# A ring of four pairs of places in a graph kernel's tile loop, with one subtraction and one row sum moved to other engines

## The chip, the cores and the metric

The kernel runs on one core of a Trainium2 chip. A core has five engines that run their own instruction streams and meet only in semaphores: PE (TensorE, matrix multiplications), DVE (VectorE), ACT (ScalarE), POOL (GpSimd) and SP (SyncE, which here only starts DMAs). PE multiplies out of SBUF into PSUM, which has eight banks; DVE and ACT bring results from PSUM back to SBUF. The metric is the time of one execution on the device, in microseconds (us), the median of several.

## The reference

Four graph layers one after the other on 3125 nodes with 128 features and 100,000 edges, sorted by destination. Layer 0 averages neighbours with edge weights in both directions, layer 1 applies the weighted adjacency three times, layer 2 the unweighted one four times, layer 3 is a message network over all edges.

```python
dst = jnp.minimum((3125 * uniform(100000) ** 2.0).astype(int32), 49999)   # sorted; crowded at the low end
...
m = ft[src] * w[:, None]                      # layer 0, both directions
msum = segment_sum(m, dst, num_segments=n); wsum = segment_sum(w, dst, num_segments=n)
...
Yk = segment_sum(edge_val[:, None] * X[edge_col], edge_row, num_segments=n)   # layer 1
...
agg = segment_sum(x[row], col, num_segments=n)                                # layer 2
```

The kernel never gathers rows for layers 0 to 2. It first builds the 3125 x 3125 matrix of edge weights (`adj`) and the matrix of edge counts (`cnt`) on the chip, and then multiplies with them. The change is in this first stage, the build.

## The kernel before

**What the build does.** Columns (destinations) are cut into 25 blocks of 125, and each block into 10 windows of 12 or 13 destinations in turn; 250 windows in all. The edges come in tiles of 128. For each tile, DVE makes two matrices by comparing an index row with a value per partition: `lanes` (L640), 128 x 128, which holds in one float both a 1 and the third part of the edge weight, and `keys` (L642), 128 x 300 or 325, a one-hot row in bf16. ACT scales `lanes` by the weight's first two parts into `scaled` (L685). PE then multiplies four times: the counts (L748), the third part of the weights (L752), and the other two parts (L756, twice), each 128 x 128 against 300 or 325 columns. All tiles of a window add up in two PSUM banks, one for counts and one for weights.

**How many tiles.** Each window has one first tile (place 0) and then a loop with a number of turns known only at run time (L514 on DVE and ACT, L543 on PE); each turn is one pair of tiles (places 1 and 2). There are 1132 tiles: 250 first ones and 441 pairs. Since destinations crowd at the low end, block 0 has 82 pairs, its first window alone 24; from block 13 on nearly every window has one pair.

**Places.** Before, even and odd windows have three places each (`SLOTS = 6`), and every place has its own `lanes`, `scaled` and `keys`. DVE may fill a place again once PE has given it free (`s_free`, raised by the last of the four multiplications). So within one window DVE is never more than two tiles ahead of PE.

**After a window.** ACT takes the counts out of PSUM as bf16 (`high`, L697) and the weights as float (L699). A count may not fit in one bf16, so PE subtracts `high` again from the PSUM bank with a multiplication by minus the identity (`rest`, L764), and ACT takes out what is left (`low`, L704), two windows behind. **After a block**, within the next block's windows: PE transposes `adj` in seven groups (L776, windows 1 to 7), which ACT copies out (L713, five groups) or DVE (L628, windows 3 and 7); PE multiplies `adj` with the node features (L784, windows 1 to 8); and DVE sums the rows of `adj` in five parts (`row_sums`, L649). SP stores the results to DRAM. POOL has nothing to do in the build.

Every engine runs the windows in the same written order; nothing is scheduled at run time but the number of turns. The blocks' loop is written out eight blocks long and turned three times.

## Time and profile before

| | us |
|---|---|
| median of 3 runs (lowest to highest) | 4106.24 (4103.90 to 4116.88) |
| span of the profiled execution | 4131.5 |
| build in it, from PE's first tile to its last | 51.0 to 1108 |
| matmul busy time, all stages | 3483.2 (84%) |
| DVE, ACT, POOL busy time | 1463.3, 1265.5, 871.1 |

For the profiled execution the trace gives its span alone, no time of its own around it; it is 25 us above the median of the runs. The page gives shares over the whole span, but the build is a stage with its own limits, so it is read in stretches, cut at block boundaries. "PEld" is PE's loading of weights; "issue" is time in which an engine waited for nothing that the profile shows, among it register and branch instructions. Such instructions are not counted as busy, but the view of one line lists them, with the letter q behind the engine (DVEq, PEldq), their number and their durations.

### The profile page before, as it was taken

Reading aid. Unit: us, or ns where it says so; the run is one execution under the profiler, and the core shown is the slowest. Engines: PE = TensorE matmul, PEld = TensorE weight load, DVE = VectorE, ACT = ScalarE, POOL = GpSimd, SP = SyncE. Lnnn points to the kernel's source line nnn. Section 1 sums busy time; section 2 is a strip of 40 time slices with the busy share of each in tenths; the row PEclk is TensorE's granted clock in tenths of the full one; section 3 lists DMA queues with packets and bytes.
Section 4 is the critical chain, followed back from the end, with each engine's and each line's share of the span. In section 5 each row is a group of like instructions: output and inputs, shape, how many; then the busy total and the mean of one; then the engine's idle time right before and its main releaser. Section 6 shows DMA issues by size and latency. Waiting matters only on the chain. (4 is left out here: it accounts for less than half of the span.)

```text
span 4131.5 us, 85615 instructions
## 1 busy us (share of the span) xinstructions
PE 3483.2 (84%) x23502; PEld 2445.5 (59%) x23503; DVE 1463.3 (35%) x4278; ACT 1265.5 (31%) x4012; POOL 871.1 (21%) x928
## 2 busy tenths in 40 slices
PE   5888889999988888968999999997777677776777
PEld 2345556777744434435999999985444445444545
DVE  6766667777601200024431111132222222222223
ACT  5566667878701300014322211232000000000001
POOL 2000000000010000000000000024666566666663
PEclk8999999999999999997999999997777778787778
DMA  2011222333495589861432222341222222222222
GB/s 60 1 46 62 69 70 87 106 101 119 133 231 127 136 188 230 196 169 31 124 107 78 76 77 77 89 115 48 65 63 63 60 63 63 62 63 63 61 63 55
DMA packets 120056, 381.79 MB, mean 92 GB/s; under 512 B 33166, under 2 KB 74620, under 8 KB 106026
## 3 DMA queue, kind: packets, MB, share of 16 engines
q1 hardware_dynamic: 90958, 324.81, 29.5%
q0 software_dynamic: 25664, 51.90, 5.7%
q8 instruction: 145, 2.38, 0.3%
q10 hardware_dynamic: 3154, 1.60, 0.2%
q14 instruction: 135, 1.11, 0.1%
HBM read 294.59 MB, written 83.62 MB: 92 GB/s over the span
## 5 line engine op out<-in xcount | busy, mean ns | idle before, releaser
L2266 POOL DMA_INDIRECT edge_rows<-src_table,src_idx x784 | 776.6, 991 | 471.2 <-issue 193.4
L685 ACT ACTIVATE build_scaled<-build_lanes,w 128x128 f32<-128x128 bf16 x1132 | 428.6, 405 | 307.4 <-DVE build_lanes L640 275.0
L756 PE MATMUL build_ps<-build_keys,build_scaled 128*128 128x300 bf16 (+1 forms) x2264 | 492.2, 299 | 20.5 <-ACT build_scaled L685 17.8
L640 DVE TENSOR_SCALAR build_lanes<-key_id,lane,one_w 128x128 f32<-128x128 f16 x1132 | 389.1, 344 | 237.9 <-PE build_ps L756 181.9
L2410 ACT ACTIVATE edge_act<-edge_ps 128x512 f32<-128x512 f32 x196 | 116.9, 597 | 1147.6 <-remote 741.7
L2382 PEld LDWEIGHTS edge_ps<-edge_hot,edge_act 128*128 128x128 f32 x1760 | 297.8, 244 | 263.5 <-issue 261.5
L1108 PE MATMUL prop_ps<-prop_rows,y 125*128 125x500 f32 (+1 forms) x1050 | 408.3, 546 | 50.0 <-DMA prop_rows<-adj_rows 43.2
L2360 PE MATMUL edge_ps<-m_store,edge_hot_t 125*128 x2640 | 269.1, 249 | 205.0 <-issue 126.0
L748 PE MATMUL build_ps<-build_keys,build_lanes 128*128 128x300 bf16 (+1 forms) x1132 | 345.3, 305 | 87.8 <-DVE build_keys L642 65.4
L642 DVE TENSOR_SCALAR build_keys<-key_id,key,win_base 128x300 bf16<-128x300 f16 (+1 forms) x1132 | 406.0, 359 | 0.5 <-issue 0.2
L2382 PE MATMUL edge_ps<-edge_hot,edge_act 128*128 x1760 | 316.3, 332 | 94.8 <-issue 58.9
L2360 PEld LDWEIGHTS edge_ps<-m_store,edge_hot_t 125*128 x2640 | 196.8, 110 | 269.2 <-issue 250.9
L1108 PEld LDWEIGHTS prop_ps<-prop_rows,y 125*128 125x128 f32 x1050 | 187.9, 191 | 269.2 <-issue 195.0
L752 PE MATMUL build_ps<-build_keys,build_lanes 128*128 128x300 bf16 (+1 forms) x1132 | 336.9, 298 | 0.0
L2368 PE MATMUL edge_ps<-edge_rows,ident 128*128 128x512 f32 x392 | 290.0, 829 | 28.7 <-issue 28.6
L756 PEld LDWEIGHTS build_ps<-build_keys,build_scaled 128*128 128x128 bf16 x2264 | 186.5, 98 | 158.4 <-ACT build_scaled L685 69.2
L748 PEld LDWEIGHTS build_ps<-build_keys,build_lanes 128*128 128x128 bf16 x1132 | 111.4, 98 | 227.0 <-DVE build_keys L642 181.2
L422 POOL DMA_DIRECT2D prop_work<-L_gnn_Wq_b_dram x1 | 0.8, 772 | 1090.3 <-POOLq L84 1090.3
L2307 DVE SCALAR_TENSOR_TENSOR edge_hot<-dst,block_base,edge_lane_id 128x500 f32 x220 | 162.8, 740 | 186.2 <-issue 177.6
L2286 DVE TENSOR_TENSOR m_agg_t<-m_agg_t,edge_ps x221 | 62.6, 283 | 459.3 <-remote 380.9
L2297 DVE TENSOR_SCALAR edge_hot_t<-edge_dst_row,block_base,edge_lane 125x512 int16 x220 | 92.6, 421 | 306.0 <-issue 176.0
L784 PE MATMUL build_ps<-h,build_adj 125*125 125x129 f32 x1250 | 173.3, 275 | 0.0
(368 smaller groups left out, 4762.4 us busy)
## 6 DMA issues: line engine op xcount, KB each, us to landing
prop_rows<-adj_rows SPq DMA_DIRECT2D x85, 1367.2 KB
cnt_panels<-build_cnt SPq DMA_DIRECT2D x50, 683.6 KB
adj_rows<-build_adj_t SPq DMA_DIRECT2D x25, 1367.2 KB
n<-cnt_panels SPq DMA_DIRECT2D x40, 683.6 KB
orders_panel<-cnt_panels SPq DMA_DIRECT2D x40, 683.6 KB
edge_dst_row<-dst_rows SPq DMA_DIRECT2D x196, 125.0 KB
h<-cnt_panels SPq DMA_DIRECT2D x20, 683.6 KB
prop_rows<-adj_rows SPq DMA_DIRECT2D x85, 158.7 KB
```

Of the source, the lines that this page charges most:

```text
L640: v.tensor_scalar(lanes[s][:], g.key_id[:, 0:128], g.lane[:, at], g.one_w3[:, at], ALU.is_equal, ALU.mult).then_inc(s_lanes[s], 1)
L642: v.tensor_scalar(keys[s][:, 0:KW[q] + q], g.key_id[:, 0:KW[q] + q], g.key[:, at], g.win_base[:, q, bass.ds(e, 1)], ALU.subtract, ALU.is_e ...
L685: a.activation(scaled[s][:], half(lanes[s], 1), ACT.Copy, scale=g.w12[:, bass.ds(t, 1)]).then_inc(s_scaled[s], 1)
L748: done = pe.matmul(ps[:, count_bank(j, parity), 0:KW[j % 2]], half(lanes[s], 1), keys[s][:, 0:KW[j % 2]], start=first, stop=False, skip_gr ...
L752: pe.matmul(ps[:, weight_bank(j), 0:KW[j % 2]], half(lanes[s], 0), keys[s][:, 0:KW[j % 2]], start=first, stop=False, skip_group_check=True)
L756: last = pe.matmul(ps[:, weight_bank(j), 0:KW[j % 2]], half(scaled[s], i), keys[s][:, 0:KW[j % 2]], start=False, stop=False, skip_group_ch ...
L784: last = pe.matmul(ps[0:B, N1, 0:D + 1], adj[parity][0:B, k, :], g.h[:, k, :], start=k == 0, stop=k == NB - 1)
L1108: last = pe.matmul(ps[:, c, 0:n * B], (y[0:B] if h else g.h)[:, row, 0:D], rows[row % R][:, b0 * B:(b0 + n) * B], start=at == 0, stop=at = ...
L2266: pool.indirect_dma_start(rows[s][:, i, :], None, dr.table, bass.IndirectOffsetOnAxis(ap=g.src_idx[:, t:t + 1], axis=0)).then_inc(s_rows[s ...
L2360: last = pe.matmul(ps[:, s, i * 128:(i + 1) * 128], hot_t[:, bass.ds(here, 1), i * 128:(i + 1) * 128] .rearrange("p a k -> p (a k)"), a3.q ...
L2368: pe.matmul(ps[:, s, :], g.ident[:], rows[s][:].rearrange("p a k -> p (a k)"), start=False, stop=True, skip_group_check=True).then_inc(s_p ...
L2382: last = pe.matmul(bank, act[s][:, i, :], hot[:, bass.ds(here, 1), i * B:(i + 1) * B].rearrange("p a k -> p (a k)"), start=i == 0, stop=i ...
```

## The change

Places 1 and 2 of the loop become a ring of four pairs that even and odd windows share: the tensors of places 1 and 2 are four times as wide, one counter goes on over all windows, and its two low bits, times 128 or 326 elements, are added to the address at run time. The first tiles keep a fixed place each for even and odd windows. The semaphore that frees a place starts at 4. `rest` on PE and `low` on ACT go; DVE instead subtracts `high` from the PSUM bank straight into the second bf16 part, behind its tiles of the window two further on. DVE's row sums go; POOL adds each finished block of `adj` to an array of 125 x 3125, and DVE sums that once at the end.

```diff
@@ build_phase
-        SLOTS = 6
-        lanes = [ph.sb(f"lanes{s}", [128, 128]) for s in range(SLOTS)]
...
+class Places:
+    def __init__(self, ph, depth):
+        self.depth = depth
+        self.lanes = [ph.sb(f"lanes{i}", [128, 128 * (depth if i > 1 else 1)]) for i in range(4)]
+        self.scaled = ...
+        self.keys = [ph.sb(f"keys{i}", [128, KEVEN * (depth if i > 1 else 1)], BF16) for i in range(4)]
+    def of(self, eng, q, place, n):
+        i = q if place == 0 else 1 + place
+        at = None if place == 0 else eng.snap(n & (self.depth - 1))
+        return i, at
...
+        SLOTS, DEPTH = 4, 4
@@ vector
-                    s = 3 * q + place
+                    s, r = places.of(v, q, place, n)
                     v.wait_ge(s_free[s], n)
-                    v.tensor_scalar(lanes[s][:], g.key_id[:, 0:128], ...
+                    v.tensor_scalar(places.wide(places.lanes[s], r), g.key_id[:, 0:128], ...
-            def row_sums(f, parity, i):
...
+            def low(w, j, parity):
+                v.wait_ge(s_high, w + 1)
+                v.tensor_tensor(in_block(cnt[parity][1], j), in_psum(count_bank(j, parity), j),
+                                in_block(cnt[parity][0], j), ALU.subtract).then_inc(s_low, 1)
...
                     spans.tiles(d, j, parity, one(j % 2, e))
+                    if j >= 2 or parity is not None:
+                        low(d * WPB + j - 2, *before(d, j, parity, 2)[:2])
...
-            v.tensor_reduce(g.wsum_src[:], rowsum[:].rearrange("p f h -> p h f"), AX.X, ALU.add)
+            v.tensor_reduce(g.wsum_src[:], by_lane[:], AX.X, ALU.add)
@@ gpsimd (new)
+            def block_of(d, parity, pair):
+                pool.wait_ge(s_weight, d * WPB + WPB)
+                pool.tensor_tensor(by_lane[:], by_lane[:], adj[parity or 0][0:B], ALU.add).then_inc(s_sum, 1)
+                pool.wait_ge(s_sum, d + 2)
+            pool.memset(by_lane[:], 0.0).then_inc(s_sum, 1)
@@ scalar
-            def low(w, j, parity):
-                a.wait_ge(s_rest, w + 1)
-                a.activation(in_block(cnt[parity][1], j), in_psum(count_bank(j, parity), j), ACT.Copy)...
@@ tensor
-                    s, first = 3 * (j % 2) + place, place == 0
+                    (s, r), first = places.of(pe, j % 2, place, n), place == 0
+                    moving = places.key(places.keys[s], r, KW[j % 2])
...
-                pe.matmul(in_psum(count_bank(j, parity), j), minus[:], in_block(cnt[parity][0], j), ...
-                pe.sem_inc(s_free[s], 1)
+                pe.sem_inc(s_free[s], DEPTH if s > 1 else 1)
```

What stands in the loop body on PE before, one turn (one pair of tiles) of an odd window. ISA and REGISTER_ALU are register instructions of PE's instruction stream; the others are as in the lines above.

```order
L55 ISA
L748 MATMUL build_ps<-build_keys,build_lanes 128x325 [waits build_keys4]
L752 MATMUL build_ps<-build_keys,build_lanes 128x325
L756 MATMUL build_ps<-build_keys,build_scaled 128x325 [waits build_scaled4]
L756 MATMUL build_ps<-build_keys,build_scaled 128x325
L748 MATMUL build_ps<-build_keys,build_lanes 128x325 [waits build_keys5]
L752 MATMUL build_ps<-build_keys,build_lanes 128x325
L756 MATMUL build_ps<-build_keys,build_scaled 128x325 [waits build_scaled5]
L756 MATMUL build_ps<-build_keys,build_scaled 128x325
L543 REGISTER_ALU
L543 COMPARE_AND_BRANCH
```

The first tile of the pair in the same place now; the second has one ISA and three REGISTER_ALU more, so a turn has ten register instructions that it did not have.

```order
L762 REGISTER_ALU [waits build_keys2]
L762 ISA x2
L762 MATMUL build_ps<-build_keys,build_lanes 128x325
L766 ISA
L766 MATMUL build_ps<-build_keys,build_lanes 128x325
L770 REGISTER_ALU [waits build_scaled2]
L770 MATMUL build_ps<-build_keys,build_scaled 128x325
L770 REGISTER_ALU
L770 MATMUL build_ps<-build_keys,build_scaled 128x325
L762 ISA [waits build_keys3]
```

The waits now stand at register instructions ahead of the multiplications. On DVE, one turn in an even window before:

```order
L640 ISA [waits build_free1]
L640 TENSOR_SCALAR build_lanes<-key_id,lane,one_w 128x128
L642 REGISTER_ALU
L642 TENSOR_SCALAR build_keys<-key_id,key,win_base 128x300
L640 ISA [waits build_free2]
L640 TENSOR_SCALAR build_lanes<-key_id,lane,one_w 128x128
L642 REGISTER_ALU
L642 TENSOR_SCALAR build_keys<-key_id,key,win_base 128x300
```

And now:

```order
L658 REGISTER_ALU [waits build_free2]
L658 ISA
L658 TENSOR_SCALAR build_lanes<-key_id,lane,one_w 128x128
L660 ISA
L660 TENSOR_SCALAR build_keys<-key_id,key,win_base 128x300
L658 ISA [waits build_free3]
L658 TENSOR_SCALAR build_lanes<-key_id,lane,one_w 128x128
L660 ISA
L660 TENSOR_SCALAR build_keys<-key_id,key,win_base 128x300
```

DVE has one register instruction more in a turn, and two of another kind; the number of its tile instructions is the same.

## Rows read from the trace of the kernel before

**Rows 1.** Whole blocks of the build: stretch, length, busy us (number) of PE, PEld, DVE, ACT...
```profile
51.00:191.50 140.50, 119.98 (x705) 47.26 (x706) 105.22 (x350) 77.23 (x209) 0.00 (x0) 0.98 0.01 4
191.50:327.00 135.50, 116.33 (x771) 63.58 (x772) 95.14 (x314) 82.15 (x242) 0.00 (x0) 1.00 0.14 47
327.00:616.90 289.90, 249.38 (x1687) 152.04 (x1688) 194.51 (x634) 185.88 (x574) 0.00 (x0) 1.00 0.20 66
616.90:757.70 140.80, 131.55 (x925) 92.72 (x925) 98.69 (x317) 103.32 (x328) 0.00 (x0) 0.98 0.28 91
757.70:1107.90 350.20, 338.21 (x2490) 262.59 (x2490) 257.61 (x818) 289.20 (x920) 0.00 (x0) 0.99 0.34 109
```

**Rows 2.** Timeline inside one window's loop: start, us, engine, line, [idle before <-releaser].
```profile
151.20 0.35 DVE L640 TENSOR_SCALAR build_lanes<-key_id,lane,one_w 128x128 f32<-128x128 f16 x1 [0.36 <-PE build_ps L756]
...
151.88 0.31 PE L748 MATMUL build_ps<-build_keys,build_lanes 128*128 128x325 bf16 x1 [0.26 <-DVE build_keys L642]
...
153.45 0.31 PE L748 MATMUL build_ps<-build_keys,build_lanes 128*128 128x325 bf16 x1 [0.24 <-DVE build_keys L642]
```

**Rows 3.** Register instructions of PE, by line: number, ns min/median/max, first and last start.
```profile
L543 PEldq COMPARE_BRANCH  x2: 215/215/215, 151.2 to 152.8; - x2
L532 PEldq FUSED_REGOPS  x122: 194/223/224, 50.6 to 1100.9; - x122
L2360 PEldq FUSED_REGOPS  x7: 46/46/51, 3006.8 to 3007.7; - x7
```

**Rows 4.** Timeline of PE at the start of block 21.
```profile
996.02 0.30 PE L748 MATMUL build_ps<-build_keys,build_lanes 128*128 128x300 bf16 x1
...
999.03 0.44 PE L764 MATMUL build_ps<-build_cnt,build_minus 128*128 128x325 bf16 x1
999.27 0.63 PE L776 MATMUL build_ps<-ident,build_adj 125*125 125x125 f32 x4
999.74 0.30 PE L748 MATMUL build_ps<-build_keys,build_lanes 128*128 128x325 bf16 x1
...
1000.85 1.05 PE L784 MATMUL build_ps<-h,build_adj 125*125 125x129 f32 x8
1001.74 0.29 PE L748 MATMUL build_ps<-build_keys,build_lanes 128*128 128x300 bf16 x1
```

**Rows 5.** The same stretch on ACT.
```profile
997.65 0.45 ACT L699 ACTIVATE build_adj<-build_ps 128x325 f32<-128x325 f32 x1
```

**Rows 6.** DVE and POOL in the setup: two timelines of one stretch.
```profile
18.57 0.61 DVE L321 TENSOR_SCALAR setup_blk<-setup_src_t 128x896 f32<-128x896 f32 x1
19.21 2.19 DVE L322 TENSOR_SCALAR setup_blk<-setup_blk 128x896 f32<-128x896 f32 x1
...
18.71 2.22 POOL L372 TENSOR_TENSOR setup_ea_left<-ea_raw,setup_ea_part 128x896 f32<-128x896 f32 x1
```

**Rows 7.** DVE's groups of the build by shape: busy us, mean ns | idle us before.
```profile
L640 DVE TENSOR_SCALAR build_lanes<-key_id,lane,one_w 128x128 f32<-128x128 f16 x1121 | 385.2, 344 | 233.8 <-PE build_ps L756 178.9 <-issue 50.4
L642 DVE TENSOR_SCALAR build_keys<-key_id,key,win_base 128x326 bf16<-128x326 f16 x561 | 203.6, 363 | 0.5 <-issue 0.2
L642 DVE TENSOR_SCALAR build_keys<-key_id,key,win_base 128x300 bf16<-128x300 f16 x561 | 198.8, 354 | 0.0
L649 DVE TENSOR_REDUCE build_rowsum<-build_adj 125x625 f32 x120 | 95.7, 797 | 0.0
```

**Rows 8.** Nearest rows for the two new operations: number, ns min/median/max.
```profile
L1334 POOL TENSOR_TENSOR x<-x,qk_half_b x1: 6950/6950/6950, 1857.9 to 1857.9; 125x3200 f32<-125x3200 f32 x1
...
L2286 DVE TENSOR_TENSOR m_agg_t<-m_agg_t,edge_ps x221: 276/284/290, 2865.3 to 4111.9; - x111
```

**Rows 9.** Waits of 616.9 to 1107.9 us: us in total, times, longest.
```profile
DVE build_adj_t L628 <- PE build_ps L776: 67.8, 26, 4.3
```

**Rows 10.** PE where the blocks' loop turns back, and the clock (third number from the end) behind it.
```profile
616.80 0.43 PE L748 MATMUL build_ps<-build_keys,build_lanes 128*128 128x300 bf16 x1 [4.25 <-issue]
...
618.00:621.00 3.00, 3.00 (x12) 1.54 (x11) 0.96 (x4) 0.40 (x1) 0.00 (x0) 0.50 0.00 0
```

More of the change, by code:

```diff
@@ L501, in __init__ @@
         self.now = [eng.alloc_register(name=f"span_now{k}") for k in range(2)]
-        self.pairs = [Counter(eng) for side in range(2)]
+        self.pairs = Counter(eng)
         eng.load(self.regs, g.spans[0:1, 0:4])
@@ L514, in tiles @@
         with self.eng.Fori(lo + 1, end, 2) as t:
-            n = self.pairs[j % 2].next()
+            n = self.pairs.next()
             one(1, t, n)
@@ L526, in __init__ @@
         self.now = eng.alloc_register(name="count_now")
-        self.pairs = [Counter(eng) for side in range(2)]
+        self.pairs = Counter(eng)
         eng.load(self.regs, g.counts[0:1, 0:4])
@@ L543, in tiles @@
         with self.eng.Fori(0, pairs):
-            n = self.pairs[j % 2].next()
+            n = self.pairs.next()
             one(1, n)
@@ L721, in block_of @@
                         out_of_psum(w - 1, jb, pb, db if parity is not None else None, pair)
-                    if j >= 2 or parity is not None:
-                        low(w - 2, *before(d, j, parity, 2)[:2])
                     if parity is not None:
@@ L732, in _ @@
             out_of_psum(NW - 1, WPB - 1, 0, None, None)
-            for j in (WPB - 2, WPB - 1):
-                low(NW - WPB + j, j, 0)
             for i in MOVES[1]:
@@ L807, in after_first @@
                     def after_first():
-                        if j >= 2 or parity is not None:
-                            rest(w - 2, *before(d, j, parity, 2)[:2])
                         if parity is not None:
@@ L825, in _ @@
             pe.drain().then_inc(s_opened, 1)
-            for j in (WPB - 2, WPB - 1):
-                rest(NW - WPB + j, j, 0)
             for j in range(1, WPB):
```

61 lines of the change are left out of this document (25 added, 36 removed).

## The prediction

> **What bounds the kernel now.** I read the busy shares in 40 slices first: in the build DVE and ACT are busy for 6 to 8 tenths and PE for 8 to 9, so none is full. Then the build in stretches of whole blocks [rows 1]. Matmuls there are four per tile, one `rest` per window and, but for the first stretch, 75 per block (25 transposes, 50 of L784). So 705 are 174 tiles; 771, 150; 1687, 294; 925, 146; 2490, 368. Less one first tile per window and halved, that is 82, 65, 117, 53 and 124 pairs, in 10, 20, 60, 40 and 120 windows.
>
> *A window with many pairs* is bound by a circle, not by an engine: DVE waits 0.36 us for PE to free a place, and PE waits 0.26 us for the keys made in it. From one pair to the next it is 151.88 to 153.45, 1.57 us for two tiles [rows 2]. Eight matmuls alone need 1.11 us (999.74 to 1000.85) [rows 4]. A ring is meant to break this circle.
>
> *A window with one pair*, as nearly all are from block 13 on, is bound by PE: 12 matmuls at 0.139 us, 1.6 to 1.7 us; on average 2.5 transposes at (0.63 - 0.27)/3 = 0.12 and 5 of L784 at (1.05 - 0.27)/7 = 0.11, 0.27 being one matmul's own time, together 0.85; and `rest` 0.24 (999.03 to 999.27) [rows 4]. That is 2.75 us; the stretch gives 350.2/120 = 2.92 [rows 1].
>
> **Part 1: the ring.** It takes the circle away, so PE gets its tiles in time. But what comes next is PE's own instruction stream. The loop body gains ten register instructions per turn. Their price: in the edge stage seven of them, and a short ALU_OP of the same line among them, start from 3006.8 to 3007.7 while PE multiplies beside them [rows 3]: seven steps, 0.13 us each. Of the ten, six are short ones, so I take 0.12. A body of 11 of them is 11 x 0.12 = 1.32 us. Turning back costs the loop's own ALU_OP and a branch of 0.215 us: from 152.8 to the next turn's first instruction some 0.3, together 0.37 us [rows 3]. A turn is 1.69 us, against 1.57 now and 1.11 of matmuls. So where a window is long the ring loses 0.12 us per turn, and where it has two or three turns it gains, since today each window also pays a start and a filling of its places.
>
> Outside the body a window has seven to eight register instructions (0.9 us), one or two of them long (0.223 against 0.046 us [rows 3]), and a register load every fourth window: 1.15 us, taken as unhidden; 0.95 in block 0. The bounds of the 0.12: 0.09, one short ALU_OP behind another, gives a body of 1.0 us, under which matmuls bound (1.11); if each of the five address ISAs took as long as L532, 0.9 us more per turn. I stay at 0.12, since L2360's are addresses for matmuls as well.
>
> PE's time by this, turns x 1.32 + turns beyond a window's first x 0.37 + windows x 1.15:
> - block 0: 108.2 + 26.6 + 9.5 = 144.3, now 140.5: +4.
> - blocks 1 to 2: 85.8 + 16.7 + 23 = 125.5, and 1 for stalls; now 135.5: -9.
> - blocks 3 to 8: 154.4 + 21.1 + 69 = 244.5, now 289.9. The blocks' loop turning back stays: 4.25 us and the half clock after it [rows 10], 5 together.
> - blocks 9 to 12: 70 + 4.8 + 46 = 120.8, and 2 for the clock; now 140.8.
> - blocks 13 to 24: a window is 1.15 + 1.32 = 2.47 by the stream and 2.5 by the matmuls; windows with transposes 2.7; I take 21.0 us for the eight windows 2 to 9.
>
> **Part 2: `rest` off PE, `low` from ACT to DVE.** PE saves 0.24 us x 250, all of it inside the numbers above, and it counts only where matmuls bind. ACT loses 250 copies; nothing waits for it then. DVE's subtraction reads 300 or 325 elements from PSUM. Between 284 ns for 125 elements [rows 8] and 797 for 625 [rows 7], 1.03 ns per element, it is 0.46 us; bounds 0.28 and 0.80. Ten per block are 4.6 us, against 5 x 0.8 = 4.0 of row sums that go. It stands behind DVE's tiles and waits for ACT's `high`, which came two windows earlier: at nothing, hidden in DVE's waits.
>
> **Part 3: the sum on POOL.** POOL itself is free. An addition of 125 x 3200 took 6.95 us [rows 8], so one of 3125 takes 6.8, 25 times, inside a block of 28 us or more. The price is what it does to DVE. In the setup the same DVE instruction took 0.61 us alone and 2.19 right after, its end (21.40) 0.47 us behind the end of POOL's addition (20.93) [rows 6]: DVE stood still until POOL was through. The tile instructions are of that kind (TENSOR_SCALAR, SBUF to SBUF), and their 128 x 326 takes only 9 ns more than 128 x 300 [rows 7], far under the 1 ns per element above. So I let POOL hold DVE for 6.8 us once per block. Bounds: nothing, if 16-bit tiles are not held, and 6.8 us on the path in each block.
>
> The Trainium skill states this as a rule (SBUF — State Buffer, "Who interferes with whom"): a DVE instruction in a mode with two ports and a GpSimd instruction exclude each other for a whole instruction, and `tensor_scalar` can enter such modes. By that rule, too, all 2264 tile instructions can be held; the trace agrees with 2.19 against 0.61 us.
>
> The hold begins when ACT has taken out a block's last weights. At block 21 that was 998.10, 2.1 us after PE opened window 0 [rows 4, 5]. With DVE ahead, PE has windows 0 and 1 to work on and then waits for window 2's keys: opening at 0, POOL from 2.0 to 8.8, keys and PE at 9.3. A block with single pairs is 9.3 + 21.0 = 30.3 us against 350.2/12 = 29.2 now. With two pairs per window the work ahead is 8 us long and hides the hold but for 1.5 us; blocks 9 to 12 lie between, 2.2 each. DVE's time for two pairs is 50 x 0.53 + 4.6 + 2.5 + 6.8 = 40.4 us, just under PE's 41. So:
> - blocks 3 to 8: 244.5 + 5 + 9 = 258.5: -31.
> - blocks 9 to 12: 122.8 + 8.8 = 131.6: -9.
> - blocks 13 to 24: 12 x 30.3 + 4 more pairs 3.6 + turning back 5.7 = 373: +23.
>
> Start and end: POOL's memset of the new array can hold DVE's first tiles, +2. The final sum over 3125 elements is about 3.3 us at 1.03 ns, beside the last stores: nothing. Clock: after 4.25 us of idleness PE ran at the lower of its levels, 1.2 GHz (0.50) [rows 10]. The new stalls of 3 to 4 us are near that; if one in three of twelve does it and costs 3 us, +12.
>
> **The sum:** 4 - 9 - 31 - 9 + 23 + 2 + 12 = -8 us. That stands against the profiled span of 4131.5 and would make 4123.5 there. The span is 25 us above the median of the runs, so in runs 4106 - 8 = 4098.
>
> **The rivals.**
> - *POOL doesn't hold the tile instructions.* For it: the row that shows a hold is of fp32 operands, the tiles read 16 bits. Against it: their short times per element. Then 9 + 9 us go in blocks 3 to 12, 45 in blocks 13 to 24 (26.5 instead of 30.3 each) and the 12 of the clock: 4098 - 75 = 4023 by full count, and as PE won't be fed without gaps, 4035.
> - *The hold finds DVE too late, and the clock falls each time* (the other side). At block 21 DVE had tiles for only part of window 1 when the weights came out. If that stays so, PE stops in window 1 from 3.9 us, goes on at 9.5 and has 1.5 + 21 left: 32.0 per block, +20 over twelve. A stall beyond 4 us then brings the half clock in each, 12 x 3 = 36 in place of 12: 4098 + 20 + 24 = 4142. It decides from blocks 13 on, if DVE's lead at a block's end is under one window. For it: DVE waits at its copies for PE's transposes (67.8 us in 26 times [rows 9]), which undoes a lead in windows 3 and 7. Against it: these waits are also slack, 4 us per block, in which the 6.8 us partly fit.
> - *Register instructions cost more.* At 0.15 a body is 1.65, +0.33 in 317 turns of blocks 0 to 12 is too much to be hidden: with a third of it, 4098 + 35 = 4133. For it: the first ISA after a wait computes two addresses. Against it: the matmuls between them ran at full pace in the edge stage.
> - *The change doesn't do what it says:* if DVE's lead stays at two tiles for another reason (first tiles still have one place per side), blocks 1 to 8 gain nothing and it is slower still; I count it with the one before.
>
> **How the numbers follow.** The forecast has 0.50, POOL holding nothing 0.15, the late hold 0.22, dearer register instructions 0.13. A measurement of this kernel tells about 0.3%, 12 us, from no change: 4094 and 4118. Of the forecast's 0.50, 0.27 lie under 4094 and 0.05 over 4118 (its own range is 4070 to 4122). Faster 0.15 + 0.27 = 0.42; slower 0.22 + 0.05 + 0.08 = 0.35; the rest 0.23. The range takes in both outer cases: 4030 to 4148.
>
> **What the changed profile would show.** In a long window the turn is near 1.69 us, PE idle for "issue" and no longer for DVE's keys, DVE waiting at L658 for a place; 1.3 would mean register instructions are cheap. One DVE instruction of about 7 us in each block, beside each addition of POOL (6.8 us); with all at 0.35, the first rival holds. PE waits for keys once per block in windows 1 or 2, blocks 13 to 24 near 30.3 us. Blocks 3 to 8 near 43 instead of 48. The subtraction near 0.46 us. I am wrong if blocks 3 to 8 don't get shorter, or the late ones don't get longer.

## The result, and the profile after

| | before | changed | |
|---|---|---|---|
| median of 4 runs (lowest to highest), us | 4105.07 (4103.03 to 4116.88) | 4156.28 (4146.07 to 4176.33) | ratio 1.0111, 95% interval 1.007 to 1.0151 |
| span of the profiled execution, us | 4131.5 | 4144.3 | |
| last tile of PE in it, us | 1107.9 | 1152.3 | +44.4 |

The changed kernel is slower by 1.1%; the forecast was 4098, with a range of 4030 to 4148. The build is 44 us longer in the profile. What comes behind it took 32 us less there (from 1127.0 to 4131.0 before, 3004; from 1172.0 to 4144.0 now, 2972), with the same instructions, so the spans show less of the difference than the medians. Whether those stages take part is what e13 below asks: within its interval they don't.

The first view is the build in stretches of whole blocks of the changed kernel, cut as in [rows 1] where PE opens a block; columns are stretch, length, busy us (number) of PE, PEld, DVE, ACT and POOL, granted clock, DMA share, GB/s.

```profile
50.70:194.40 143.70, 109.20 (x697) 66.80 (x698) 106.83 (x372) 76.39 (x209) 0.00 (x0) 0.98 0.01 4
194.40:320.20 125.80, 106.94 (x752) 74.54 (x751) 108.21 (x328) 75.08 (x220) 13.60 (x2) 1.00 0.16 51
320.20:585.50 265.30, 227.63 (x1627) 168.85 (x1626) 230.14 (x651) 167.60 (x508) 40.72 (x6) 0.96 0.22 73
585.50:736.30 150.80, 126.33 (x885) 95.76 (x885) 126.10 (x337) 93.55 (x289) 27.27 (x4) 0.91 0.26 85
736.30:1152.30 416.00, 332.70 (x2370) 259.55 (x2369) 341.39 (x876) 254.30 (x798) 81.44 (x12) 0.91 0.28 92
```

| blocks | before [rows 1] | after | difference | predicted |
|---|---|---|---|---|
| 0 | 140.5 | 143.7 | +3.2 | +4 |
| 1 to 2 | 135.5 | 125.8 | -9.7 | -9 |
| 3 to 8 | 289.9 | 265.3 | -24.6 | -31 |
| 9 to 12 | 140.8 | 150.8 | +10.0 | -9 |
| 13 to 24 | 350.2 | 416.0 | +65.8 | +23 |

The reader is to see two things: the first three terms are close (the third by 6 us), the last two are far off, and the clock column, at 0.96 in the third, falls to 0.91 where they are. The rows sum to +44.7.

**The long loop**, where [rows 2] showed 1.57 us from pair to pair: PE and DVE now, and PE's register instructions of two lines from 60 to 64 us.

```profile
61.73 0.30 PE L762 MATMUL build_ps<-build_keys,build_lanes 128*128 x1 [0.46 <-DVE build_keys L660]
...
63.39 0.30 PE L762 MATMUL build_ps<-build_keys,build_lanes 128*128 x1 [0.46 <-DVE build_keys L660]
```

```profile
61.07 0.34 DVE L658 TENSOR_SCALAR build_lanes<-key_id,lane,one_w 128x128 f16 x1 [0.20 <-issue]
...
62.41 0.35 DVE L658 TENSOR_SCALAR build_lanes<-key_id,lane,one_w 128x128 f16 x1 [0.20 <-PE build_ps L770]
```

```profile
L762 PEldq FUSED_REGOPS  x8: 37/37/79, 60.0 to 63.8; - x8
...
L543 PEldq COMPARE_BRANCH  x2: 208/208/208, 61.0 to 62.7; - x2
```

A turn of PE is 63.39 - 61.73 = 1.66 us; DVE, still filling the ring here, makes a pair in 62.41 - 61.07 = 1.34. So DVE is the faster, and the releaser named for PE's 0.46 us, the keys, is only the instruction that came last by the profile; the gap is the branch and the address computations ahead of the first matmul (one row names "issue" for the same 0.46).

**A late block.** Around the end of block 20, with block 21 opened by PE at 1016.46: PE, then DVE, then POOL, each from its own timeline, then the granted clock.

```profile
1018.68 0.30 PE L762 MATMUL build_ps<-build_keys,build_lanes 128*128 128x325 bf16 x1 [0.46 <-issue]
...
1019.23 0.60 PE L784 MATMUL build_ps<-ident,build_adj 125*125 125x125 f32 x4
1025.28 0.45 PE L762 MATMUL build_ps<-build_keys,build_lanes 128*128 x1 [5.45 <-DVE build_keys L660]
...
1027.43 1.40 PE L792 MATMUL build_ps<-h,build_adj 125*125 125x129 f32 x8
1028.67 0.29 PE L762 MATMUL build_ps<-build_keys,build_lanes 128*128 128x300 bf16 x1
```

```profile
1017.80 0.34 DVE L658 TENSOR_SCALAR build_lanes<-key_id,lane,one_w 128x128 f16 x1
1018.06 6.85 DVE L660 TENSOR_SCALAR build_keys<-key_id,key,win_base 128x326 f16 x1
```

```profile
1018.04 6.77 POOL L692 TENSOR_TENSOR build_by_lane<-build_by_lane,build_adj 125x3125 f32<-125x3125 f32 x1 [28.44 <-ACT build_adj L722]
```

```profile
1020.00:1022.00 2.00, 0.00 (x0) 0.00 (x0) 2.00 (x1) 0.00 (x0) 2.00 (x1) 0.83 0.00 0
1022.00:1024.00 2.00, 0.00 (x0) 0.00 (x0) 2.00 (x1) 0.00 (x0) 2.00 (x1) 0.50 0.00 0
...
1026.00:1028.00 2.00, 2.00 (x10) 1.44 (x8) 2.00 (x9) 1.94 (x7) 0.00 (x0) 0.50 0.64 192
```

POOL starts at 1018.04. DVE's next instruction, which else takes 0.36 us, takes 6.85. At that moment DVE was making the first pair of window 1, and PE opened window 1 only 0.64 us later: the lead was about half a window. It was like this in all twelve blocks 13 to 24: when the addition starts, DVE is at window 1 and PE in window 0. PE used up what there was and stopped for 5.45 us (from 1019.83). When it went on, the clock was at the lower level (0.50, 1.2 GHz): from 1025.28 to 1028.67, 3.39 us for eight matmuls and the eight of L792; the same sixteen at the higher level take 2.00 (e14 below). So 1.4 us more behind this stop. Two more views, of the whole stretch of 195 to 1150 us and of the addition's line:

```profile
PE build_ps L762 <- DVE build_keys L660: 111.8, 48, 6.0
```

```profile
L692 POOL TENSOR_TENSOR build_by_lane<-build_by_lane,build_adj x25: 6760/6779/6917, 195.9 to 1153.9; 125x3125 f32<-125x3125 f32 x25
```

PE waits 111.8 us for keys, and each of the 24 additions that fall within the tile loops has one tile instruction of DVE of 6.4 to 7.0 us beside it. In blocks 1 to 3, where the windows have more pairs, PE doesn't stop for over 1.1 us beside them; in blocks 13 to 24 it stops for 4.4 to 6.0 us beside eleven of the twelve, and for 3.0 beside the other. Beside the 25th, at 1153.9, DVE copied a group of transposes out of PSUM in its usual 0.68 us.

### The profile page after: what moved, and what is told of

The parts are those of the page before. It is cut to its first block and busy times, and to the rows that moved or that the text cites. A ratio compares the mean times of both kernels' runs of the same rounds, so it can differ in the third digit from the quotient of the medians.

```text
span 4144.3 us, 90845 instructions
## 1 busy us (share of the span) xinstructions
PE 3424.9 (83%) x23252; PEld 2489.4 (60%) x23253; DVE 1624.7 (39%) x4402; ACT 1193.3 (29%) x3762; POOL 1038.6 (25%) x954
## 3 DMA queue, kind: packets, MB, share of 16 engines
q14 instruction: 141, 1.15, 0.1%
## 5 line engine op out<-in xcount | busy, mean ns | idle before, releaser
L708 ACT ACTIVATE build_scaled<-build_lanes,w (+1 forms) x1132 | 424.7, 400 | 372.8 <-DVE build_lanes L658 316.4
L762 PE MATMUL build_ps<-build_keys,build_lanes 128*128 (+1 forms) x1132 | 348.4, 308 | 212.1 <-DVE build_keys L660 144.4
L658 DVE TENSOR_SCALAR build_lanes<-key_id,lane,one_w 128x128 f16 (+1 forms) x1132 | 470.5, 416 | 124.7 <-issue 59.4
L770 PE MATMUL build_ps<-build_keys,build_scaled 128*128 (+1 forms) x2264 | 503.7, 305 | 0.0
L660 DVE TENSOR_SCALAR build_keys<-key_id,key,win_base 128x300 f16 (+2 forms) x1132 | 476.4, 421 | 0.6 <-issue 0.2
L2386 PEld LDWEIGHTS edge_ps<-edge_hot,edge_act 128*128 128x128 f32 x1760 | 292.1, 239 | 265.3 <-issue 264.1
L2364 PE MATMUL edge_ps<-m_store,edge_hot_t 125*128 x2640 | 270.8, 251 | 192.9 <-issue 143.6
L692 POOL TENSOR_TENSOR build_by_lane<-build_by_lane,build_adj 125x3125 f32<-125x3125 f32 x25 | 169.8, 6794 | 940.5 <-ACT build_adj L722 940.5
L766 PE MATMUL build_ps<-build_keys,build_lanes 128*128 (+1 forms) x1132 | 345.4, 305 | 0.0
L2372 PE MATMUL edge_ps<-edge_rows,ident 128*128 128x512 f32 x392 | 291.4, 832 | 24.0 <-issue 21.9
L762 PEld LDWEIGHTS build_ps<-build_keys,build_lanes 128*128 (+1 forms) x1132 | 112.5, 99 | 326.0 <-issue 282.4
L770 PEld LDWEIGHTS build_ps<-build_keys,build_scaled 128*128 (+1 forms) x2264 | 225.5, 100 | 75.3 <-issue 0.9
L792 PE MATMUL build_ps<-h,build_adj 125*125 125x129 f32 x1250 | 187.8, 290 | 0.0
```

The lines of the kernel that those rows point to most:

```text
L658: v.tensor_scalar(places.wide(places.lanes[s], r), g.key_id[:, 0:128], g.lane[:, at], g.one_w3[:, at], ALU.is_equal, ALU.mult).then_inc(s_ ...
L660: v.tensor_scalar(places.key(places.keys[s], r, KW[q] + q), g.key_id[:, 0:KW[q] + q], g.key[:, at], g.win_base[:, q, bass.ds(e, 1)], ALU.s ...
L708: a.activation(places.wide(places.scaled[s], r), places.narrow(places.lanes[s], r, 1), ACT.Copy, scale=g.w12[:, bass.ds(t, 1)]).then_inc(s ...
L762: done = pe.matmul(ps[:, count_bank(j, parity), 0:KW[j % 2]], places.narrow(places.lanes[s], r, 1), moving, start=first, stop=False, skip_ ...
L766: pe.matmul(ps[:, weight_bank(j), 0:KW[j % 2]], places.narrow(places.lanes[s], r, 0), moving, start=first, stop=False, skip_group_check=True)
L770: last = pe.matmul(ps[:, weight_bank(j), 0:KW[j % 2]], places.narrow(places.scaled[s], r, i), moving, start=False, stop=False, skip_group_ ...
```

## The experiments

Theory H: POOL's addition holds DVE's tile instruction for its whole length when DVE's lead is short; PE stops, and its clock falls. The rivals are named where they are tested: register instructions (R), contention by bytes (C), the ring's length (D), the lead doesn't matter (L).

Runs e1 to e15 were taken in four sessions in which the kernel before takes 3864 to 3866 us; e16 in one where it takes 4094, near the result's 4105. So the comparison is by ratio to the kernel before in the same session, and by the build's stretches, which differ little from session to session (the changed kernel's, in two profiles: 143.7 and 143.6, 125.8 and 125.8, 265.3 and 265.6, 150.8 and 150.4). "13-23" is to the opening of block 24. All stretches are from the view of stretches, cut where PE opens a block. e1 and e8 show how far two sessions can be compared: their builds agree to 0.2 us up to block 24, their ratios differ by 0.0032.

| kernel | ratio to before (95%) | 0 | 1-2 | 3-8 | 9-12 | 13-23 |
|---|---|---|---|---|---|---|
| before | 1 | 140.6 | 135.4 | 289.9 | 140.9 | 322.3 |
| changed | 1.0111 (1.007 to 1.0151) | 143.7 | 125.7 | 265.4 | 150.8 | 381.8 |
| e13 changed, again | 1.0107 (1.0079 to 1.0135) | 143.6 | 125.8 | 265.6 | 150.4 | 383.5 |
| e1 without POOL | 0.9826 (0.9793 to 0.9859) | 144.0 | 123.9 | 242.6 | 128.3 | 312.0 |
| e2 ring alone | 0.9883 (0.9854 to 0.9913) | 143.4 | 124.0 | 244.3 | 136.0 | 330.4 |
| e3 subtraction alone | 0.9887 (0.9865 to 0.9909) | 136.2 | 129.7 | 270.1 | 135.0 | 310.9 |
| e4 POOL sum alone | 1.0409 (1.0387 to 1.043) | 140.4 | 149.2 | 329.7 | 167.8 | 391.9 |
| e5 POOL in pieces | 0.9856 (0.9804 to 0.9908) | 143.9 | 123.8 | 244.2 | 131.5 | 320.1 |
| e6 POOL, one partition | 1.0168 (1.0134 to 1.0202) | 145.9 | 125.7 | 266.1 | 155.5 | 386.5 |
| e8 no POOL, depth 2 | 0.9794 (0.9765 to 0.9822) | 143.7 | 123.1 | 242.9 | 129.1 | 312.2 |
| e9 changed, copy on ACT | 1.0009 (0.9984 to 1.0034) | 143.6 | 126.4 | 252.7 | 141.7 | 363.0 |
| e10 no POOL, copy on ACT | 0.978 (0.9747 to 0.9813) | 144.1 | 124.4 | 245.3 | 125.3 | 302.6 |
| e11 addresses alone | 1.0045 (1.0024 to 1.0066) | 166.0 | 144.6 | 285.8 | 138.0 | 315.1 |
| e14 stop filled, 44 matmuls | 1.0345 (1.0319 to 1.037) | 143.0 | 140.2 | 294.4 | 165.0 | 411.8 |
| e16 stop filled, 24 matmuls | 1.01 (1.0066 to 1.0135) | 142.9 | 131.8 | 269.0 | 148.2 | 369.0 |
| e15 as e10, depth 2 | 0.9754 (0.9716 to 0.9793) | 144.1 | 124.4 | 245.1 | 125.7 | 302.6 |

**The parts one by one: e1 to e4.** e1 is the changed kernel with this undone:

```diff
-            def block_of(d, parity, pair):                 # POOL
-                pool.wait_ge(s_weight, d * WPB + WPB)
-                pool.tensor_tensor(by_lane[:], by_lane[:], adj[parity or 0][0:B], ALU.add).then_inc(s_sum, 1)
+                        if j in SUM_AT:                    # DVE, as before
+                            row_sums(d - 1, 1 - parity, SUM_AT.index(j))
```

e2, e3 and e4 are the kernel before with one part of the change each: the ring, the subtraction on DVE, the sum on POOL.

> The changed kernel with the row sums back on DVE (five reductions per block) and nothing on POOL; ring and DVE's subtraction stay. Theory H (POOL's addition holds DVE for 6.8 us per block when DVE has almost no lead, PE stops 5 to 6 us and then runs at half clock): window 1 of a late block took 10.0 us in place of 2.4 to 2.7; without the hold 12 late blocks give back 7.5 each = 90, less what five reductions of 0.8 us cost where DVE is near its limit (up to 2 us a block), four blocks 9 to 12 some 6 each, blocks 3 to 8 some 2 each: 4156 - 90 - 24 - 12 + 20 = about 4050, clock in the build 0.98 to 1.00. Rival R (register instructions of the ring are what costs): within 15 us of the changed kernel, 4140 to 4160.

> The kernel before with the ring of four pairs alone; the subtraction stays on PE and ACT, the row sums on DVE. Theory H: turn of the long loop 1.66 us in place of 1.57 (block 0 +3), blocks 1 and 2 -10, blocks 3 to 8 about -30, blocks 9 to 12 -8, late blocks within 1 us of 29.2 each: 4105 - 45 = about 4060. Rival R: late blocks 31 us or more each, so 4105 or slower.

> The kernel before with the subtraction of the counts' second part on DVE alone (no ring, no POOL). PE loses 0.24 us per window: where PE is the bound (blocks 9 to 24, 160 windows) up to -38 us. Where the circle of DVE and PE is the bound (blocks 0 to 8, 90 windows) DVE's 0.47 us stand between a window's last tile and the next first one, up to +0.4 each, +36 us. Theory H: between 4075 and 4115, late blocks shorter than 29.2, early ones longer. Rival R says nothing of it.

> The kernel before with the row sums on POOL alone: no ring, subtraction on PE and ACT. Theory H: DVE has two tiles of lead at most, so the 6.8 us of each of 24 blocks land on PE, with half clock behind (about 1.9 us): 24 x 6 to 8 less what DVE's five reductions cost before (up to 2 a block): 4105 + 100 to 170 = 4205 to 4275, clock in the build about 0.91. Rival R: POOL's part costs nothing, 4095 to 4110.

Measured in medians against 3864.6: e1 3801.56 (-63), e2 3827.88 (-37), e3 3823.38 (-41), e4 4025.44 (+161). The stretch of blocks 13 to 23, of e1 and then of e4, and PE's wait for keys in e1 over 195 to 1150 us:

```profile
688.50:1000.50 312.00, 287.63 (x2178) 225.12 (x2179) 277.55 (x864) 234.61 (x735) 0.00 (x0) 0.99 0.35 113
```

```profile
840.40:1232.30 391.90, 334.26 (x2289) 256.56 (x2287) 273.46 (x699) 268.24 (x846) 74.90 (x11) 0.92 0.27 89
```

```profile
PE build_ps L768 <- DVE build_keys L661: 21.9, 40, 1.5
```

So ring and subtraction are both gains, and the sum on POOL costs more than the two bring. Without it PE's wait for keys is 21.9 us instead of 111.8 and the clock stays at 0.99. Rival R (register instructions are what makes the change slower) is out. One miss: e3's early blocks didn't get longer by DVE's 0.47 us per window but shorter (289.9 to 270.1 in blocks 3 to 8). What there outweighs DVE's added work, PE's `rest` or ACT's copy and its wait, was not taken apart.

**How the hold comes about: e5, e6, e7 and e12.** e5 cuts the addition, e6 puts one on a single partition into e1, e7 makes all element counts of DVE's tile instructions odd, e12 measures forms by themselves.

```diff
 e5
+                for i in range(5):
+                    at = slice(5 * i, 5 * i + 5)
+                    if i:
+                        pool.wait_ge(s_opened, d * WPB + (WPB + 2 * i + 2))
+                    pool.tensor_tensor(by_lane[:, at], by_lane[:, at], adj[parity or 0][0:B, at], ALU.add).then_inc(s_part, 1)
 e6
+                pool.wait_ge(s_weight, d * WPB + WPB)
+                pool.tensor_tensor(scr[0][:], scr[0][:], scr[1][:], ALU.add)     # 1 x 3125
 e7
-                    v.tensor_scalar(places.wide(places.lanes[s], r), g.key_id[:, 0:128], ...
+                    v.tensor_scalar(places.wide(places.lanes[s], r, 130, 129), g.key_id[:, 0:129], ...
```

> The changed kernel with POOL's addition cut into five of 125 x 625, the first when the block's weights are out, the others when windows 3, 5, 7 and 9 of the next block are opened. The same sum, the same number of elements. Theory H: five holds of about 1.36 us instead of one of 6.8; PE never stops for 4 us in a block, the granted clock stays at 1.00 but where the loop turns back, late blocks 27 to 29 us instead of 34.7; the whole within 30 us above e1 (no POOL at all), so 0.982 to 0.991 of before. Rival C (POOL's access slows DVE by contention in proportion to its bytes, or the total of the hold is what counts): DVE still loses 6.8 us per block, blocks stay at 32 us or more, 1.00 or more of before.

> e1 (ring, DVE's subtraction, row sums on DVE) with an addition on POOL at the place where the changed kernel has it, of 3125 elements on one partition of two tiles of its own; it adds to the work and its result is not used. Theory H (the hold is by instruction, not by bytes): POOL needs the same 6.8 us, DVE has one instruction of about 6.8 us per block again, time as the changed kernel or up to 2 us a block more: 1.011 to 1.02 of before. Rival C (contention by bytes, 1/125 of them): no DVE instruction over 1 us, time as e1, 0.983.

> The changed kernel with an odd number of elements in every tile instruction of DVE (129 instead of 128 for the lanes, whose places are 130 wide, 301 and 325 instead of 300 and 326 for the keys), POOL's addition as it is. Theory H in its narrow form (DVE is held because its tile instructions run in a fast form that uses both ports, which needs an even count): each tile instruction becomes longer (keys 0.36 to 0.5 us or more), but none in the 24 additions is held for over 1 us, and PE's stops of 5 to 6 us go. If DVE is held whatever its form: still 24 instructions of 6.8 us.

> e1 with a measurement ahead of the build: ten times POOL does a long instruction (eight additions of 128 x 3125, then two memsets of that size) and DVE beside it does one form twice: the lanes' instruction as it is; the same with constants instead of scalars in SBUF; fp32 whose source has an outer dimension of 5 with gaps; the source in PSUM; a copy; an addition of two SBUF operands; the subtraction from PSUM; a reduction; then beside the memsets the addition and the copy. Theory P (a fast form with both ports is what is held): the first two and the copies are held until POOL is through, 6.8 us; PSUM, reduction and subtraction take their 0.3 to 0.5 us. If the scalars in SBUF were the cause, the second is not held. Not known: the gapped one and the addition.

e5 first: its blocks 13 to 23, and one of its additions.

```profile
695.00:1015.10 320.10, 290.83 (x2177) 226.28 (x2177) 279.91 (x807) 232.35 (x734) 84.00 (x55) 0.98 0.34 110
```

```profile
967.68 1.51 POOL L697 TENSOR_TENSOR build_by_lane<-build_by_lane,build_adj 125x625 f32<-125x625 f32 x1 [5.51 <-PE build_ps L768]
```

POOL works longer than before (84.0 us for 55 pieces against 74.7 for 11 whole ones), and the kernel is 0.9856 instead of 1.0111 of before. So not the sum of the holds counts, but whether one hold is longer than DVE's lead. e6, whose addition has 1/125 of the bytes, on POOL and then on DVE:

```profile
990.23 6.76 POOL L711 TENSOR_TENSOR build_scr<-build_scr 1x3125 f32<-1x3125 f32 x1 [27.52 <-ACT build_adj L742]
```

```profile
990.26 6.84 DVE L663 TENSOR_SCALAR build_keys<-key_id,key,win_base 128x326 f16 x1
```

Same duration, same hold, same loss: contention by bytes (rival C) is out twice. e7 told nothing of what it was made for: 24 instructions were held for 6.4 to 6.9 us again, but the 301 and 325 wide keys took 350 to 366 ns in block 0 as the 300 and 326 wide ones had (346 to 370), so the edit didn't change the form in which DVE runs them. Its time was 3923.68 in a single run. e12 has the forms. DVE's rows first (each form is issued twice, and a row is both), then three of POOL's ten:

```profile
53.65 13.80 DVE L675 TENSOR_SCALAR build_f32c<-key_id,lane,one_w 128x128 f32<-128x128 f16 x2 [3.24 <-POOLq L748]
67.48 6.92 DVE L676 TENSOR_SCALAR build_f32c<-key_id 128x128 f32<-128x128 f16 x2
74.44 1.02 DVE L677 TENSOR_SCALAR build_f32c<-build_f32a 128x325 f32<-128x325 f32 x2
75.50 1.27 DVE L678 TENSOR_SCALAR build_f32c<-build_ps,lane,one_w 128x325 f32<-128x325 f32 x2
81.44 7.13 DVE L679 COPY build_f32c<-build_f32a 128x326 f32<-128x326 f32 x2 [4.68 <-POOLq L748]
88.61 14.04 DVE L680 TENSOR_TENSOR build_f32c<-build_f32a,build_f32b 128x325 f32<-128x325 f32 x2
102.69 1.03 DVE L681 TENSOR_TENSOR build_f32c<-build_ps,build_f32b 128x325 f32<-128x325 f32 x2
103.75 1.02 DVE L682 TENSOR_REDUCE build_f32c<-build_f32a 128x5 f32<-128x325 f32 x2
109.45 1.03 DVE L683 TENSOR_TENSOR build_f32c<-build_f32a,build_f32b 128x325 f32<-128x325 f32 x2 [4.68 <-POOLq L748]
112.31 3.23 DVE L684 COPY build_f32c<-build_f32a 128x326 f32<-128x326 f32 x2 [1.83 <-POOLq L748]
```

```profile
74.50 6.76 POOL L750 TENSOR_TENSOR build_scr<-build_scr 128x3125 f32<-128x3125 f32 x1 [0.18 <-POOL build_scr L750]
...
109.43 2.70 POOL L752 MEMSET build_scr<- 128x3125 f32 x1 [0.15 <-POOL build_scr L750]
112.28 2.70 POOL L752 MEMSET build_scr<- 128x3125 f32 x1 [0.15 <-POOL build_scr L752]
```

Held beside POOL's additions (the first eight rows; the seventh and eighth stand beside one from 102.48 to 109.28): the lanes' instruction and the addition of two SBUF operands, both instances (13.80 and 14.04 us for two); the same with constants and the SBUF copy, one instance of two (6.92 and 7.13 us), as the first one got through when an addition of POOL's was about to start. Not held: a source with gaps (0.51 us each), a source in PSUM although its scalars are in SBUF, the subtraction from PSUM, the reduction. Beside a memset, which only writes, the addition runs freely and the copy is held. (e12's own time is from a single run, 3845.89, and tells nothing here.) So theory P stands, and the scalars in SBUF are not the cause. The ten rows agree with what the Trainium skill states (SBUF — State Buffer, "Who interferes with whom"): forms with two ports are locked out for a whole POOL instruction, two-operand forms by POOL's reads alone, reductions never.

**Ring and register instructions: e8 and e11.** e8 is e1 with `SLOTS, DEPTH = 4, 2`. e11 is e3 with run-time addresses on PE that always give the same place:

```diff
+                    at = None if first else pe.snap((n >> 20) & 1)
+                    moving = keys_w[s][:, 0:width] if at is None else keys_w[s][:, bass.ds(at * KEVEN, width)]
```

> e1 (no POOL) with a ring of two pairs of places instead of four. Theory H: a turn stays at 1.66 us, since PE's register instructions bound it, and two pairs of lead are enough where no hold has to be bridged: within 8 us of e1. Rival D (the ring's length is what brings blocks 1 to 8 their gain): blocks 3 to 8 back towards 290 us in all from 242, 30 us or more over e1.

> e3 (DVE's subtraction alone, six fixed places) with PE's addresses of places 1 and 2 computed at run time as in the ring, but always to the same place: 11 register instructions more per turn on PE and no place more for DVE. Theory H (PE's register instructions bound the turn of the ring): a turn of the long loop at least 1.66 us in place of 1.54, and up to 1.9, since those between the wait and the first matmul (about 0.3 us) stand inside the circle with DVE; block 0 from 136 to 146 to 162 us, the whole 1.00 to 1.03 of before against e3's 0.989. If register instructions are hidden beside matmuls: block 0 stays under 139.

PE in the long loop, e8, then e3 (fixed addresses), then e11:

```profile
60.63 0.30 PE L768 MATMUL build_ps<-build_keys,build_lanes 128*128 x1 [0.46 <-issue]
...
62.30 0.30 PE L768 MATMUL build_ps<-build_keys,build_lanes 128*128 x1 [0.47 <-issue]
```

```profile
60.68 0.30 PE L742 MATMUL build_ps<-build_keys,build_lanes 128*128 128x300 bf16 x1 [0.19 <-DVE build_keys L637]
...
62.22 0.30 PE L742 MATMUL build_ps<-build_keys,build_lanes 128*128 128x300 bf16 x1 [0.19 <-DVE build_keys L637]
```

```profile
60.68 0.30 PE L752 MATMUL build_ps<-build_keys,build_lanes 128*128 x1 [0.73 <-DVE build_keys L639]
...
62.61 0.30 PE L752 MATMUL build_ps<-build_keys,build_lanes 128*128 x1 [0.74 <-DVE build_keys L639]
```

Two pairs of places do what four do: a turn of 1.67 us against 1.66, 242.9 us in blocks 3 to 8 against 242.6. Rival D is out. The addresses by themselves make a turn 1.93 instead of 1.54 us and block 0 166.0 instead of 136.2, a little beyond the 162 expected. In the ring these instructions no longer stand in the circle with DVE, and the turn is what PE's own stream needs.

**The lead: e9 and e10.** Both let ACT copy out the last group of transposes; e9 is the changed kernel, e10 is e1.

```diff
-        MOVES = [[2, 6], [0, 1, 3, 4, 5]]
+        MOVES = [[2], [0, 1, 3, 4, 5, 6]]
```

> The changed kernel with the last group of transposes copied out by ACT instead of DVE (window 7), so that DVE waits for PE's transposes once per block (window 3) and not twice. Theory H (the hold is dear because DVE's lead when it comes is under one window): DVE wins about 0.5 us a window on PE, so two to three more windows of lead-building give 1 to 2 us; late blocks from 34.7 to 32 to 33.5, the whole 15 to 40 us below the changed kernel, 0.998 to 1.007 of before. Rival L (the lead doesn't matter, or is set elsewhere): within 8 us of the changed kernel, 1.010 to 1.014.

> The control to the last: e1 (no POOL) with the same copy on ACT. No hold, so lead buys nothing: within 8 us of e1, 0.981 to 0.985 of before, by theory H as by rival L.

DVE in e9 at one of the holds (block 23 opened by PE at 1047.34), and the stretch of blocks 13 to 23 in e9:

```profile
1048.35 0.50 DVE L667 TENSOR_TENSOR build_cnt<-build_ps,build_cnt 128x325 bf16<-128x325 f32 x1
1049.01 6.61 DVE L658 TENSOR_SCALAR build_lanes<-key_id,lane,one_w 128x128 f32<-128x128 f16 x1 [0.16 <-issue]
```

```profile
715.40:1078.40 363.00, 303.27 (x2178) 236.85 (x2179) 309.42 (x795) 235.51 (x745) 74.76 (x11) 0.93 0.30 97
```

One wait of DVE less per block, and here the hold finds DVE with all of window 1 made; PE's stop is 3.1 us and no longer 5.6. But this holds for seven of the twelve blocks 13 to 24 alone. In the other five DVE is still in window 1, as in the changed kernel, and PE stops for up to 5.3 us. The changed kernel goes from 1.0107 to 1.0009 of before; the same edit without POOL from 0.9826 to 0.978, intervals that just overlap. That was expected to be within 8 us of e1 and is 9 us less in the build, so the copy on ACT brings something without a hold too. Beside POOL it brings 41 us in the build (1068.9 to 1027.4 up to block 24), and the difference, some 32 us, is what DVE's longer lead takes off the price of the hold. The lead decides the price of the hold: theory H, not L.

**Stop and clock: e13, e14, e16.** e13 is the changed kernel unedited. e14 and e16 put matmuls that nothing reads where PE would stop, 44 or 24 of them:

```diff
+                            if j == 1:
+                                for k in range(44):
+                                    pe.matmul(ps[0:B, weight_bank(1), 330:459], adj[1 - parity][0:B, k % NB, :],
+                                              g.h[:, k % NB, :], start=False, stop=False, skip_group_check=True)
```

> The changed kernel unedited, on the chip that the experiments ran on, where the kernel before takes 3865 us and not 4105. Its build was 1113 us against 1068 in the first two profiles (+45). If the whole effect lies in the build, it is 3865 + 45 = about 3910, 1.009 to 1.015 of before. If the stages behind the build take part (their profiles differed by 32 us the other way), it comes out elsewhere.

> The changed kernel with 44 matmuls of 125x129 on PE behind the transposes of window 1 (some 4.8 us, into columns of the window's weight bank that nothing reads; work added that the output doesn't need), so that PE is busy where it would stop for the hold. The hold itself stays. Theory H with the clock as a term of its own: the granted clock no longer falls in windows 1, the eight matmuls and the eight of the node features behind the stop go at full clock, 1.3 us less per block, 24 blocks: 20 to 35 us below the changed kernel on the same chip, 1.002 to 1.007 of before, though PE has 115 us more work. If the fall of the clock is only a companion and costs nothing: the same as the changed kernel or slower.

> e14 with 24 matmuls in place of 44. In e14 they ran as 88 passes for 9.9 us, twice what was meant, and outlasted the stop, so that it did not tell; 24 are 48 passes, 5.4 us at e14's 0.11 each, about the length of the stop (5.2 to 6). The hold stays. If the half clock is a term of its own: window 1 of a late block 8.6 us instead of 10.0, 24 blocks by 1.3 = 20 to 35 us below the changed kernel, 1.002 to 1.007 of before, with clock 0.99 in the blocks 13 to 24. If it costs nothing: 1.011 or more.

e13: 3909.82 against 3865.19, +45 us (by its interval 31 to 52), as the build. So the loss lies there, as far as this interval tells. e14 missed through my sizing: each fp32 matmul stands in the trace as two (44 issued, x88) and takes the time of both, so the filling outlasted the stop.

```profile
1062.72 9.90 PE L820 MATMUL build_ps<-h,build_adj 125*125 125x129 f32 x88
1072.46 0.30 PE L762 MATMUL build_ps<-build_keys,build_lanes 128*128 x1
...
1073.58 1.05 PE L792 MATMUL build_ps<-h,build_adj 125*125 125x129 f32 x8
1074.46 0.29 PE L762 MATMUL build_ps<-build_keys,build_lanes 128*128 128x300 bf16 x1
```

Yet it shows the work behind the stop at full clock, 1072.46 to 1074.46: 2.00 us against 3.39. e16 in blocks 13 to 23:

```profile
743.10:1112.10 369.00, 346.53 (x2705) 283.49 (x2705) 314.31 (x808) 232.99 (x734) 75.15 (x11) 0.99 0.29 96
```

With the hold as it was and 5.4 us of matmuls more per block, these eleven blocks take 369.0 instead of 381.8 to 383.5 us, 1.2 to 1.3 us less each, at clock 0.99 instead of 0.91. The ratio of the whole, 1.01, doesn't show it, against the 1.002 to 1.007 that were expected: in blocks 1 to 8, where the stop is shorter than the filling, e16 takes 9 to 10 us more. So the half clock costs what the rows say in the late blocks; for the whole kernel the split rests on the rows.

**The fastest version: e15**, e10 with two pairs of places.

> e10 (ring, DVE's subtraction, row sums on DVE, last copy on ACT) with a ring of two pairs instead of four: the candidate for the fastest version. As e10 within 8 us, 0.976 to 0.981 of before.

3773.42 against 3865.19. From e10 it is not to be told apart (0.9754 and 0.978). e15 beats the kernel before by 2.1 to 2.8%, e10 by 1.9 to 2.5%; the changed kernel, at 1.0107, is over 3% slower than both.

## Why the prediction was wrong

- *The bound of the long windows, and the turn of the ring.* Right. 1.69 us was predicted, 1.66 measured, DVE no longer the limit (1.34), block 0 +3.2 for +4, blocks 1 and 2 -9.7 for -9. e11 shows that register instructions cost, as the step said. That four pairs were more than needed it didn't see.
- *`low` on DVE, 0.46 us.* Right in size (456/478/502 ns in the late blocks). But the step said that what PE is spared counts only where matmuls bind. Part 2 alone is -41 us (e3), 20 of them in blocks 3 to 8, where the circle was said to bind. Where the ring is there already, it adds less (e2 to e1, -26).
- *The hold: 6.8 us, once per block, on DVE's tile instructions.* Right: POOL's addition takes 6.76 to 6.92 us, the instruction held 6.4 to 7.0, and the first rival (POOL holds nothing) was wrong. The step was argued from one row [rows 6]; e12 shows that the form decides.
- *Where the hold finds DVE.* **This is the step that failed.** "With DVE ahead, PE has windows 0 and 1 to work on and then waits for window 2's keys." In the trace POOL's 6.77 us begin in the middle of DVE's work on window 1. With window 1's keys missing PE stops 1.15 us after it has opened that window, for 5.45 us and not for the 3 to 4 supposed in the sum. The lead was assumed, not worked out. The trace shows what takes it: in window 7 of block 20 DVE waits 0.93 us for PE's transposes (copied at 1008.78), and in window 9 it makes no tile for 1.41 us, while its instruction stream loads registers, from 1011.78 on:

```profile
1013.60 0.34 DVE L658 TENSOR_SCALAR build_lanes<-key_id,lane,one_w 128x128 f16 x1 [1.41 <-issue]
```

```profile
L513 DVEq TENSOR_LOAD <-spans x1: 1270/1270/1270, 1011.8 to 1011.8; - x1
```

At 1014.72 PE waits 0.91 us for keys, so hardly any lead is left before block 21 begins. A load of 1.26 or 1.27 us stands at this place, 6 to 10 us ahead of the hold, before six of the twelve late holds, every second one; the kernel's other loads mostly take 0.35. What it is worth no run tells, since none takes it out. The second rival said that the hold would find DVE too late, with the condition ("under one window") and the sign, and had 0.22. Its time, 4142, was 14 us short: it has 32.0 us per late block, and 416.0/12 is 34.7.

- *The clock.* 12 us in the sum, for one stop in three of twelve, at 3 us each. The number of falls was wrong more than their price (1.3 to 3.0 us, half of what PE is busy in each). Each late block has a fall, and eight of the blocks 4 to 12. By the clock column the changed kernel runs (0.04 x 265.3 + 0.09 x 150.8 + 0.09 x 416.0)/0.5 = 123 us at the lower level, the kernel before 13. In narrow stretches of the trace these are 21 falls up to the opening of block 24, each of 3.4 or 6.8 us (the one above from 1021.3 to 1028.1), where the kernel before has two, behind the turning back of the loop. Within the 21 PE is busy for 82 us, within e1's two for 7. At full clock that work takes half, so the falls cost 41 us at most, against 4: 37 more. That is an upper bound, since DVE catches up while PE is slow. With PE's wait for keys (110.6 us in e13 up to block 24, 20.5 in e1) it makes 90 and up to 37 us. To the opening of block 24 e13 and e1 differ by 1068.9 - 950.8 = 118, in medians by 108.
- *Blocks 9 to 12,* -9 predicted and +10 measured, and blocks 3 to 8, -31 and -24.6: the same mistake. e1 has 128.3 and 242.6 there, against the 122.8 and 249.5 that the sum had without a hold.
- *Start and end.* The memset cost nothing on the path (first tile at 50.7, before 51.0), for +2; the final sum 3.40 us, as said, beside other work.

The gains were nearly right and so was the mechanism of the loss; a lead of one window too much turned -8 into +45 to +51.

## What to carry to other kernels

Before moving work to POOL, ask which form DVE's instructions have beside it: an SBUF to SBUF `tensor_scalar`, copy or two-operand addition that came second stood still until POOL's whole addition was through (e12), and the addition's length was the same on one partition (e6). What it costs is set by the longest single hold against the lead that DVE has at that moment; so read the lead from the timeline (which window is each engine in?), in several blocks and not in one, cut the instruction into pieces, and take out waits that undo the lead. A ring with run-time addresses is paid for in register instructions, here PE's (e11); a depth of two may do all that a depth of four does (e8).

## What the runs showed of the hardware that was not expected

- POOL's fp32 addition takes 6.76 us for 3125 elements on one partition as on 125 (e6), and five pieces of 625 take 1.51 each, 7.6 together.
- A DVE copy of fp32 is held beside a POOL memset too (3.23 us for two, the memset 2.70), the addition of two SBUF operands only beside POOL's addition (1.03 against 14.04 for two, e12). The reader of a trace sees it only as a long DVE instruction; no wait is reported.
- An odd element count, equal at source and destination, changes neither DVE's durations nor the hold (e7); a source of 5 x 65 with a gap after each 65 takes 0.51 us for 325 elements and isn't held (e12). The Trainium skill has both (VectorE: DVE Perf Modes, "Mode 2×_2P"): the outer dimension has to be even, or odd and equal on both sides.
- The same kernel differs by 6% between sessions (4105 and 3865 us for the kernel before). The two profiles of the changed kernel put all of it behind the build: 2972 us there at a granted clock of 0.89, 2731 in e13 at 0.94 (1173.5 to 3904). Whether the chip is the cause isn't shown: e13 to e15 and e16 have the same chip number on record, at 3865 and 4094 us for the kernel before.
- DVE's load of registers from SBUF (`TENSOR_LOAD`, L513) takes 339 to 1379 ns in the late blocks, most of them 346, and with a long one DVE makes no tile for 1.4 us. What makes some long was not looked into.
